# One transfer for the experts' empty rows, and idle products in TensorE's first pauses: a decoder layer on one core

## The reference

```python
x = x + attn(layernorm(x), W_qkvb, W_o, ln_g, ln_b)      # scan over time: W += beta * (v - W k) k^T; out = W q
x = x + xattn(layernorm(x), ctx, Wq, Wk, Wv, Wout, bout)
x = x + ffn(layernorm(x), router_w, w1, w2)

# ffn: capacity C = 256 rows for each of the 8 experts
expert_idx = argmax(softmax(x_flat @ router_w))
pos = cumsum(onehot(expert_idx))[own expert] - 1; keep = pos < C
expert_in = zeros((E, C, D)).at[expert_idx, pos_c].add(x_flat * keep[:, None])
hidden = gelu(einsum('ecd,edf->ecf', expert_in, w1))
expert_out = einsum('ecf,efd->ecd', hidden, w2)
y = expert_out[expert_idx, pos_c] * (gate * keep)[:, None]
```

## Time and profile before

| | |
|---|---|
| median of three runs | 1326.24 us (1325.76 to 1326.59) |
| profiled execution, its own time | 1325.07 us |
| its span in the profile | 1323.3 us, so 1.8 us lie around it |
| mean granted TensorE clock | 0.991 |
| busy share | PE 97%, DVE 78%, POOL 69%, ACT 68% |
| instructions | 22,939 |

### The profile page before, as it was taken

The page is one execution under the profiler, slowest core; times in us unless marked ns, Lnnn a source line. Parts: engine busy times, 40 slices in busy tenths (PEclk is TensorE's granted clock), DMA queues, the critical chain, the costliest instruction groups (busy, mean ns, idle before and its releaser), DMA issues. The chain is left out here.

```text
span 1323.3 us, 22939 instructions
## 1 busy us (share of the span) xinstructions
PE 1277.5 (97%) x8470; PEld 1073.1 (81%) x8470; DVE 1037.7 (78%) x1656; ACT 898.1 (68%) x1322; POOL 913.9 (69%) x652
## 2 busy tenths in 40 slices
PE   5899999999999999999999999999999999888998
PEld 4688888888887778888888888888888888777997
DVE  6355498859316889999999999999999999985554
ACT  5555433425646787878878888778788778675774
POOL 2544410225410799999999999999999989763553
PEclk9999999999999999999999999999999999997999
DMA  6702032146764989888888889888888888786671
GB/s 220 105 6 75 3 104 81 57 130 248 209 224 143 240 203 234 213 210 221 213 216 215 205 210 230 206 207 227 207 214 211 212 205 210 176 253 250 203 242 60
DMA packets 172379, 241.37 MB, mean 182 GB/s; under 512 B 34179, under 2 KB 78085, under 8 KB 172272
## 3 DMA queue, kind: packets, MB, share of 16 engines
q1 hardware_dynamic: 155040, 208.11, 62.5%
q10 hardware_dynamic: 15184, 25.96, 5.6%
q0 software_dynamic: 2048, 5.90, 1.1%
HBM read 64.79 MB, written 41.32 MB: 80 GB/s over the span
## 5 line engine op out<-in xcount | busy, mean ns | idle before, releaser
L1244 POOL TENSOR_TENSOR xa_pT<-xa_moved,xa_pT 128x1024 fp32r<-128x1024 f32 x246 | 588.0, 2419 | 14.2 <-ACT xa_pT L1782 14.0
L1594 PE MATMUL xa_S<-xa_kT,xa_qT 128*128 128x512 f32 x1536 | 379.4, 395 | 2.5 <-ACT xa_probs L1788 2.5
L1613 PE MATMUL xa_O<-xa_pT,xa_v 128*128 128x512 f32 x1536 | 376.7, 394 | 3.3 <-DVE xa_pT L1419 2.6
L1788 ACT ACTIVATE xa_probs<-xa_S,xa_mx_nb_rinv 128x1024 f32<-128x1024 f32 x256 | 286.1, 1118 | 137.3 <-DVE xa_mx_nb_rinv L1366 137.3
L1613 PEld LDWEIGHTS xa_O<-xa_pT,xa_v 128*128 128x128 f32 x1536 | 289.0, 189 | 69.9 <-POOL xa_pT L1244 3.5
L1594 PEld LDWEIGHTS xa_S<-xa_kT,xa_qT 128*128 128x128 f32 x1536 | 284.8, 188 | 66.9 <-ACT xa_probs L1788 4.6
L1363 DVE TENSOR_REDUCE xa_mx_nb_rinv<-xa_S 128x1 f32<-128x1024 f32 x256 | 302.7, 1209 | 45.7 <-PE xa_S L1594 45.7
L1376 DVE STREAM_TRANSPOSE xa_tq<-xa_probs 128x1024 f32<-128x1024 f32 x256 | 316.8, 1238 | 15.7 <-ACT xa_probs L1788 8.2
L1782 ACT ACTIVATE xa_pT<-xa_moved 128x1024 fp32r<-128x1024 f32 x254 | 253.9, 1050 | 4.1 <-DMA heads_q<-ci_outs 2.4
L506 PE MATMUL fw_pp<-fw_hT,fw_wqk 128*128 128x512 f32 x384 | 94.8, 404 | 4.4 <-DVE fw_hT L647 4.4
L506 PEld LDWEIGHTS fw_pp<-fw_hT,fw_wqk 128*128 128x128 f32 x384 | 73.1, 194 | 20.8 <-DVE fw_hT L647 3.0
(11 more groups left out here) (255 smaller groups left out, 1782.7 us busy)
## 6 DMA issues: line engine op xcount, KB each, us to landing
xa_moved<-xa_tq SPq DMA_DIRECT2D x508, 256.0 KB, 4.6
heads_k<-ci_outs SPq DMA_DIRECT2D x32, 256.0 KB, 2.1
heads_v<-ci_outs SPq DMA_DIRECT2D x32, 256.0 KB, 2.3
heads_q<-ci_outs SPq DMA_DIRECT2D x32, 256.0 KB, 2.2
xa_rawv<-heads_v ACTq DMA_DIRECT2D x32, 256.0 KB, 4.3
ex_w1s<-in_L_ffn_w_dram SPq DMA_DIRECT2D x8, 1024.0 KB, 7.0
ex_w2s<-in_L_ffn_w_dram SPq DMA_DIRECT2D x8, 1024.0 KB, 9.3
xa_rawq<-heads_q ACTq DMA_DIRECT2D x31, 256.0 KB, 4.3
```

Source lines behind the costliest of these rows:

```text
L1244: pool.tensor_tensor(quadrants(pT[LO], r), unit_moved(r), quadrants(pT[HI], r).bitcast(F32), ALU.subtract).then_inc(lo_ready, 1)
L1594: last = pe.matmul(banks[:, k % 2], qT[a][:, i // GT % 2, q], kT[b][h % 2][:, k * 512:(k + 1) * 512], start=(n == 0), stop=(n == 2))
L1613: last = pe.matmul(O[:], v[a][:, j * P:(j + 1) * P], pT[b][:, r % PRING, k], start=(j == 0 and n == 0), stop=(j == JT - 1 and n == 2))
L1788: act.activation(probs[:, unit % RING], S[:, score_banks(unit)].rearrange("p a b -> p (a b)"), ACT.Exp, bias=nb[:, s % 2:s % 2 + 1], scale ...
```

## The change

Three edits, all in `fast_weight_block`.

1. `nobody` (128 x 2) becomes `blank` (128 x 514): POOL sets its first 512 columns to 0.0 and the last two to 4096, so one memset more, and `id_ready` counts to 4.
2. SP fills `expert_in` with one transfer of 2,048 rows of 2,056 bytes from `blank`, issued right behind the load of `wo`, once `blank` is there. It no longer waits for the splits. The five transfers of before are gone. `filled` is waited for with 16 at the end of the block.
3. PE makes idle products (`keep_busy`: `ident` by `ident` into a bank that is overwritten later): 24 ahead of its first transposes, and 6 behind the transposes of the second half, once the first of these banks has been read by DVE's split.

```diff
-        nobody = sb("fw_nobody", [P, 2])
+        blank = sb("fw_blank", [P, ROW])
@@ sync
-            sp.wait_ge(id_ready, 3)
-            sp.wait_ge(hT_ready, TILES // 2)
-            slots = xe.rearrange("(p r) d -> p r d", p=P)
-            for c in range(0, GATE, P):
-                sp.dma_start(slots[:, :, c:c + P], ident[:].unsqueeze(1).to_broadcast([P, E * CAP // P, P])) \
-                    .then_inc(filled, 16)
-            sp.dma_start(slots[:, :, GATE:ROW], nobody[:].unsqueeze(1).to_broadcast([P, E * CAP // P, ROW - GATE])) \
-                .then_inc(filled, 16)
+            sp.wait_ge(id_ready, 4)
+            sp.dma_start(xe.rearrange("(p r) d -> p r d", p=P),
+                         blank[:].unsqueeze(1).to_broadcast([P, E * CAP // P, ROW])).then_inc(filled, 16)
@@ end of sync
-            sp.wait_ge(filled, 16 * (GATE // P + 1))
+            sp.wait_ge(filled, 16)
@@ gpsimd
-            pool.memset(nobody[:], float(2 * TOK)).then_inc(id_ready, 1)
+            pool.memset(blank[:, 0:GATE], 0.0).then_inc(id_ready, 1)
+            pool.memset(blank[:, GATE:ROW], float(2 * TOK)).then_inc(id_ready, 1)
@@ tensor
+            def keep_busy(n, bank):
+                for _ in range(n):
+                    pe.matmul(bank, ident[:], ident[:], start=True, stop=True)
+
             pe.wait_ge(id_ready, 2)
+            keep_busy(24, gr[:, 1, 1, 0:P])
             for j in range(4):
                 transpose_h(j)
@@
                 if i == 1:
                     for j in range(4, TILES // 2):
                         transpose_h(j)
+                    pe.wait_ge(hT_ready, T // 2 + 1)
+                    keep_busy(6, gr[:, 0, 0, 0:P])
```

## The result

| | before | after |
|---|---|---|
| median | 1326.24 us, five runs 1323.6 to 1327.5 | 1316.81 us, five runs 1315.4 to 1318.3 |
| ratio, after to before | | 0.9932, 95% interval 0.9917 to 0.9946 |
| profiled execution | 1325.07 us | 1316.23 us |
| its span | 1323.3 us | 1314.5 us |
| mean granted clock | 0.991 | 0.995 |

The change is faster by 9.4 us between the medians; 6.4 us were forecast. The time lies 0.6 us under the range.

What follows compares the result with a forecast made beforehand. The prediction took PE's own path from 10.6 to 54 us as what the change can reach. It summed 5.4 (hole) + 1.0 (idle products) = 6.4 us, forecasting 1319.8 us against the median, range 1317.4 to 1323.

Steps and rivals of the forecast that it cites:

- The hole: PE's 3.4 us stop in the second gram pair: instructions held up by the fill; removing it gains 5.4 us.
- 1.0 us for the 24: Idle products ahead of PE's first transposes raise the clock early, so the third projection starts sooner: 1.0 us, ends 0 and 1.25.
- "Zero" for the 6: Idle products ahead of the third projection fill a PE pause and keep the clock where otherwise in doubt: no gain.
- Before, the pause of 2.81 us cost no clock: PE's pause ahead of the third projection: the 24 products behind it took 5.73 us, so no clock was lost.
- step 2: Start of PE's third projection, at 27.79 us before; forecast at 26.5 to 27 us after the change.
- the lower case: The clock falls in the pause ahead of the first projection, leaving 0.8 us of the early idle products' gain.
- what is gained there should go through to the end: Time gained on PE's own path from 10.6 to 54 us should reach the program's end.
- rival 1: Part of the gain is given back in the head or later: 1321.5 to 1323.5 us; chance 0.17.
- The median to start from: The forecast was raised 1.2 us from the profiled execution's basis to the runs' median, 1318.7 to 1319.8 us.
- The signs that were named: No hole before 60 us, gram period about 7.7 us, full clock, idle products over by 10.6, later grams at about 47.8.
- Rival 4: Larger gain, because the profile missed small holes the fill made in 33 to 54 us: 1317.5 us; chance 0.06.
- Rival 3: Slower: fetches wait longer because 2,056-byte pieces hold an engine four times as long as 512-byte ones; 1330.2 us; chance 0.04.

Runs made afterwards that it cites:

- fill_only: The changed kernel without its 24 and 6 idle products, so the early fill in one transfer alone; ratio to the kernel before 0.9972.
- after_again: Unchanged copy of the changed kernel, profiled and timed again; ratio to the kernel before 0.9945.
- idle_only: The kernel before with the 24 and 6 idle products added and its own old fill; ratio to the kernel before 0.9966.
- five_early: The kernel before with its five fill transfers issued at the new, earlier time, no idle products; ratio to the kernel before 0.9984.
- after_3: Unchanged copy of the changed kernel, profiled and timed a third time; ratio to the kernel before 0.9941.
- one_late: The changed kernel without idle products, its one fill transfer started at the old time behind the splits; ratio to the kernel before 0.9976.
- before_again: Unchanged copy of the kernel before, profiled and timed again; ratio to the kernel before 0.9988.
- before_3: Unchanged copy of the kernel before, profiled and timed a third time; ratio to the kernel before 0.9997.

## Why the prediction was wrong

*The hole: right in mechanism; its size was one execution's.* The fill starved PE of instructions, and the change took that away. 5.4 us is what it is worth in the profiled pair; four executions of before's head give 0.5 to 5.9, 3.5 in the mean, and the runs 3.7 (fill_only). So this term was 1.7 us too large.

*The failed step: the idle products, 1.0 us for the 24 and "Zero" for the 6.* Together they were sized at 1.0 us. The runs give 8.1 - 3.7 = 4.4 us for the two (with some 2.5 us to either side); in one set alone, after_again is 4.1 us (2.4 to 5.9) faster than fill_only. So this term was 3.4 us too small. "Before, the pause of 2.81 us cost no clock" was true of the execution that I had, and I made the cover of it a rule. The pause costs the clock in four of nine executions. The 24 were sized at 1.0 and brought 1.7 us at step 2 in the profile after, 0.6 and 0.5 in its repeats: what I named as the lower case (the clock falls ahead of step 0, 0.8 us) is what two of three executions show. What the head shows for both adds to 1.2 to 2.4 us, and 1.6 by the start of the first grams over seven profiles each. The rest of the 4.4, some 2 to 3 us, is within its error or in the end of the program; no experiment shows which.

*The step "what is gained there should go through to the end".* It went through whole to 1184 us: rival 1, part given back, is refuted but for the 0.42 us for POOL. Even that is for the most part not the memset's: idle_only and five_early, which have the short memset of before, wait 0.28 and 0.23 us at the same place. What is late next when the hole goes is POOL's preparation of weights, and I had not named it. I had not thought that the end varies by itself: the clock falls or not in the router's pauses, and the rest ranges from 1119.1 to 1125.0 us over the profiles. The 2.2 us that the profile after gained there lie within that; in after_3 they are not there. The mean of the rest over the six profiles without any idle products added is 1122.6, over the seven with both sets and none in the router 1121.0; the scatter in each is some 1.8, so whether the products move the end at all stays open.

*The median to start from.* A forecast in microseconds leaned on three runs of before; its sets range from 1324.0 to 1328.1. By the mean of the three ratios the changed kernel stands at 1318.1 for 1326.24, inside the range; the set that decided was the best for it of the three. So of the 3.0 us by which the forecast was off, 1.7 are mis-sized terms (3.4 for the idle products less 1.7 for the hole, which partly hid each other) and 1.3 the spread between sets. The hit in the profiled pair, 5.4 us against 5.4, was luck in so far as another execution of before would have given 2.3 or 0.5.

*The signs that were named.* No hole, period 7.68, traffic to 33 us, 16 transposes in 2.60, idle products over by 9.9: as written. Step 2 at 26.07 (26.5 to 27 forecast) and grams at 47.11 (47.8) came sooner by the mis-sized 0.7 us. The half clock between 20 and 60 us did not occur. Rival 4 had the right side, not the reason: no small holes were missed. Rival 3 took the time of a piece to go with its size, four times as long; in the traces a piece of 2,056 bytes takes 0.11 us in the mean (after) and one of 512 takes 0.05 (before), about twice. One correction to the text ahead of the prediction: the experts' block does loop over its experts; the head has no loop.

*What stays open.* Why the clock rises at different moments from one execution to the next, and with it where it falls; why the fetch under the old fill comes 3.4 us late in one and 8.0 in another; why the sets of the kernel before differ on one chip (1324.3, then 1328.1); which part of the 4.4 us belongs to which set; and why the kernel with the old fill and all idle products stays behind the change in time but not in its profiles.

## What to carry to other kernels

A pause with the releaser "issue" in a stretch of small instructions, while a large transfer runs, points to a starved instruction queue: see whether its packets come late, and whether the engine goes on behind the end of one. Move the transfer; moving the instructions moves the hole. A cost or a cover that hangs on the granted clock is not to be taken from one profile: take several executions of the kernel before (four gave a hole of 0.27 to 3.40 us here), look at each pause, and price it by when the next stage starts over all of them, since a clock that falls late may have risen early. And the untouched rest of a long program moves by itself by as much as a small gain: widen the range for it.

## What the runs showed of the hardware

- A refill of instructions (16 KB, one packet of about 1 us) ran 2.65 us after the start of the first grams when no transfer was in the way (fill_only), 4.0 us later under pieces of 2,056 bytes (one_late), and 3.4 to 8.0 us later under pieces of 512 (four executions of before's head). PE went on 1.3 to 1.4 us behind the end of a late packet (before, before_again, before_3).
- The same 4.2 MB took SP 13.30 us to issue in four parts of 512-byte rows, and 3.32 us in one of 2,056-byte rows. In that form it ran some 13 us (from the end of the loads near 20 to 32.5), where the five parts of before ran from 27.82 to beyond 50.
- A hole of 2.03 us left the clock up, one of 3.29 or 3.40 us did not; but pauses of 2.75 to 2.93 us went either way: behind them step 2 took 7.10 to 7.38 us in four executions and 5.73 or 5.74 in five.
- The time of a run goes with its mean granted clock: over 128 runs of the kernel before, 1.07 us less for each 0.001 more, with a correlation of -0.79; over 17 of the changed one, 0.71 us and -0.90. So some three fifths of the spread in the times of before goes with the clock; which of the two moves the other is not shown.
